# Cross attention: each score tile moved one slot ahead, evictions put before exponents, dense products moved with them

## The reference

```python
# x: (2, 2048, 512), ctx_1024: (2, 154, 512), 16 heads of 32
def _layernorm(x): return (x - mean(x)) / sqrt(var(x) + 1e-5)
q = (_layernorm(x) @ Wq.T + bq)          # heads of 32
k = (ctx @ Wk.T + bk);  v = (ctx @ Wv.T + bv)
attn = softmax(q @ k.T / sqrt(32))       # per head, over 154 keys
x = x + (attn @ v) @ Wo.T + bo
x = x + ffn(_layernorm(x))               # ffn: two layers of local attention + gated MLP
```

## Time and profile before

| | us |
|---|---|
| median of 3 runs | 3729.19 (3726.97 to 3729.65) |
| the profiled execution, its own time | 3725.76 |
| its span, first to last instruction | 3724.0 |
| cross attention groups, about | 63 to 642 of the span |
| TensorE busy over the span | 3486.6 (94%) |

### The profile page before, as it was taken

One profiled execution on the slowest core, in us unless ns is written; L12 is line 12 of the kernel. 1 busy time (PEld: TensorE's weight loads), 2 busy tenths in 40 slices (PEclk: granted clock), 3 DMA queues, 4 the chain that ended last, 5 costly groups with the idle time before them and its releaser, 6 DMA issues. The chain is left out here.

```text
span 3724.0 us, 56508 instructions
## 1 busy us (share of the span) xinstructions
PE 3486.6 (94%) x20624; PEld 2821.9 (76%) x20624; DVE 2267.6 (61%) x5002; ACT 1504.1 (40%) x3973; POOL 1177.3 (32%) x1036
## 2 busy tenths in 40 slices
PE   5889987799999997999999969999999699999998
PEld 4666665688888875888888858888888588888887
DVE  5776775699999984322332239999999642322221
ACT  4655663455555553111111125555555421111111
POOL 2333342555555531111111125555555111111111
PEclk8999999899999998999999989999999899999999
DMA  5111122212121114111111121211111231111111
GB/s 132 39 42 54 56 76 70 92 61 64 60 63 58 58 51 139 66 63 63 63 63 62 52 103 51 63 59 58 58 58 56 89 112 62 63 63 63 63 62 52
DMA packets 215591, 249.21 MB, mean 67 GB/s; under 512 B 32761, under 2 KB 142594, under 8 KB 215317
## 3 DMA queue, kind: packets, MB, share of 16 engines
q1 hardware_dynamic: 215317, 245.61, 20.3%
HBM read 138.17 MB, written 90.61 MB: 61 GB/s over the span
## 5 line engine op out<-in xcount | busy, mean ns | idle before, releaser
L1674 DVE SCALAR_TENSOR_TENSOR u_full<-banks,b_cols,gate 128x512 f32<-128x512 f32 (+1 forms) x176 | 132.1, 751 | 890.8 <-ACT gate L1616 793.2
L45 PE MATMUL banks<-fxT_h,w_h 128*128 128x512 f32 (+1 forms) x1408 | 558.3, 397 | 5.2 <-DVE fxT_l L1666 5.2
L47 PE MATMUL banks<-fxT_h,w_l 128*128 128x512 f32 (+1 forms) x1408 | 557.3, 396 | 0.0
L46 PE MATMUL banks<-fxT_l,w_h 128*128 128x512 f32 (+1 forms) x1408 | 556.5, 395 | 0.0
L1616 ACT ACTIVATE gate<-banks,b_cols 128x512 f32<-128x512 f32 (+1 forms) x176 | 121.3, 689 | 1028.8 <-PE banks L47 1028.8
L1010 POOL TENSOR_TENSOR rn<-ssq,neg_half 128x8 f32<-128x8 f32 x128 | 210.8, 1647 | 410.7 <-DVE ssq L1282 404.2
L45 PE MATMUL banks<-wqkv_h,hT_h 128*128 128x512 f32 x768 | 323.3, 421 | 16.1 <-DVE wqkv_l L1269 16.1
L1323 DVE TENSOR_SCALAR prob<-prob,rc 128x384 f32<-128x384 f32 (+2 forms) x512 | 315.6, 658 | 9.1
L45 PEld LDWEIGHTS banks<-fxT_h,w_h 128*128 128x128 f32 (+1 forms) x1408 | 260.3, 185 | 75.7 <-DVE fxT_l L1666 11.1
L1218 ACT ACTIVATE pT_h<-banks 128x384 fp32r<-128x384 f32 (+2 forms) x512 | 213.7, 469 | 254.3 <-PE banks L1107 253.5
L47 PEld LDWEIGHTS banks<-fxT_h,w_l 128*128 128x128 f32 (+1 forms) x1408 | 261.2, 186 | 67.6
(11 more groups left out here) (170 smaller groups left out, 8195.4 us busy)
## 6 DMA issues: line engine op xcount, KB each, us to landing
y_in<-y_rows SPq DMA_DIRECT2D x64, 256.0 KB, 2.9
z_rows<-y_in SPq DMA_DIRECT2D x64, 256.0 KB, 2.0
f_res<-z_rows SPq DMA_DIRECT2D x16, 1024.0 KB, 5.6
f_x<-x_rows SPq DMA_DIRECT2D x16, 1024.0 KB, 8.0
y_rows<-f_res SPq DMA_DIRECT2D x16, 1024.0 KB, 4.3
out_rows<-f_x SPq DMA_DIRECT2D x16, 1024.0 KB, 4.8
w_ffn_stage<-in_w SPq DMA_DIRECT2D x30, 512.0 KB, 4.9
x_in<-in_x SPq DMA_DIRECT2D x10, 1024.0 KB, 6.7
```

The source lines that it names most:

```text
L45: pe.matmul(out, a_h, b_h, start=start, stop=False)
L46: pe.matmul(out, a_h, b_l, start=False, stop=False)
L47: return pe.matmul(out, a_l, b_h, start=False, stop=stop)
L1674: e.scalar_tensor_tensor(out=u_full[r, m % 2, :], in0=ps[r, 2 * (m % 2), :], scalar=b1[r, m, 0:1], in1=gate[r, :], op0=ALU.add, op1=ALU.mu ...
```

## The change

The scores of tile k+1 (not k) of quarter q+1 stand in slot (q, k), and tile 0 of quarter q+2 stands in slot (q, 4) behind the values product, so that the first tile of a quarter comes one slot sooner. The maxima and exponents are moved with them. In each slot ACT now does `hi_q`, `hi_p` and `hi_x` ahead of the exponents; before, the exponents of tile 0 stood ahead of `hi_p`. The dense products are now at Q2 (0,1), P0 at the end of (0,2), P1 (0,3), P2 (0,4), P3 (1,0), Q3 (1,2), TX0 at the end of (1,3), TX1 at the end of (1,4), TX2 at the end of (2,0), TX3 (2,1), Q0 (2,2), Q1 (3,2). On DVE, normalise moves to (0,1) and (0,2), moments to (3,2) and (3,4), and all four finish instructions stand together at (1,2). SP sends the first half of the second batch's keys ahead of the stores of that group. No instruction is added or taken away in the groups.

```diff
@@ -397,11 +397,13 @@
                 def body(g, s):
                     if g.first:
                         return
+                    if s == XSLOTS - 1:
+                        e.wait_ge(pe_s, NS * g.it + GT * K_HALVES[0][1])
+                        load_keys(1, 0)
                     store_before(g, g.it)
                     if s == XSLOTS - 1:
-                        for half, (_, c1) in enumerate(K_HALVES):
-                            e.wait_ge(pe_s, NS * g.it + GT * c1)
-                            load_keys(1, half)
+                        e.wait_ge(pe_s, NS * g.it + GT * K_HALVES[1][1])
+                        load_keys(1, 1)
                         for half, (_, c1) in enumerate(V_HALVES):
                             e.wait_ge(pe_o, DC * g.it + c1)
                             load_values(1, half)
@@ -547,33 +549,24 @@
                     for q in range(DC):
                         for k in range(QK):
                             m = QK * q + k
-                            if k < GT and not (g.last and q == DC - 1):
-                                if (q, k, s) == (DC - 1, 0, XSLOTS - 1):
-
-                                    e.wait_ge(ld_k[0], g.turn * K_LOADED + 2 * K_LOADED)
-                                if (q, k) == (1, 0):
-                                    reloaded(ld_k[1], K_LOADED)
-                                scores(it, q + 1, k)
+                            if k < GT - 1 and not (g.last and q == DC - 1):
+                                scores(it, q + 1, k + 1)
                             transpose_p(it, m)
-                            if (q, k) == (0, 1) and not g.first:
-
-                                e.wait_ge(dv_o, DC * it)
-                                project(0, TURNS, q_out(2))
-                            elif (q, k) == (0, 2) and not g.first:
+                            if (q, k) == (0, 1):
+                                queries(2, q_out(2))
+                            elif (q, k) == (0, 3) and not g.first:
...
                                 values(it, m - 2)
@@ -582,8 +575,22 @@
                                 if k == 2 and q in (0, DC - 1):
                                     reloaded(ld_v[q // (DC - 1)], V_LOADED)
                                 values(it, m - 2)
-                            if (q, k) == (1, 4) and not g.last:
+                            if k == GT and not (g.last and q >= DC - 2):
+
+                                if (q, s) == (DC - 2, XSLOTS - 1):
+                                    e.wait_ge(ld_k[0], g.turn * K_LOADED + 2 * K_LOADED)
+                                if q == 0:
+                                    reloaded(ld_k[1], K_LOADED)
+                                scores(it, q + 2, 0)
+                            if (q, k) == (0, 2) and not g.first:
+                                e.wait_ge(dv_o, DC * it)
+                                project(0, TURNS, q_out(3))
+                            elif (q, k) == (1, 3) and not g.last:
                                 transpose_x(it + 1, 0, TURNS, q_out(4))
+                            elif (q, k) == (1, 4) and not g.last:
+                                transpose_x(it + 1, 1, TURNS, x_out(1))
+                            elif (q, k) == (2, 0) and not g.last:
+                                transpose_x(it + 1, 2, TURNS, x_out(2))
 
                 def nothing():
                     pass
@@ -598,6 +605,7 @@
                 queries(1, nothing)
                 scores(0, 0, 2)
                 scores(0, 0, 3)
+                scores(0, 1, 0)
                 for half in ld_v:
                     e.wait_ge(half, V_LOADED)
                 run(e, body)
@@ -641,19 +649,18 @@
                     for q in range(DC):
                         more = not (g.last and q == DC - 1)
                         for k in range(QK):
-                            if k == 0 and q != 2 and more:
-                                exps(it, q + 1, k)
                             if k == 1 and not (g.first and q == 0):
                                 hi_o(it, q - 1)
+                            if k == (2 if q == 0 else 3) and (q < 2 or not g.last):
+                                hi_q(it, q + 2)
                             hi_p(it, QK * q + k)
-                            if (q, k) == (1, 4) and not g.last:
-                                hi_x(it + 1, 0, TURNS)
-                            elif q == 2 and k < 3 and not g.last:
-                                hi_x(it + 1, k + 1, TURNS)
-                            if (0 < k < GT or (q, k) == (2, 0)) and more:
-                                exps(it, q + 1, k)
-                            if k == 3 and (q < 2 or not g.last):
-                                hi_q(it, q + 2)
+                            x_of = {(1, 3): 0, (1, 4): 1, (2, 0): 2, (2, 1): 3}.get((q, k))
+                            if x_of is not None and not g.last:
+                                hi_x(it + 1, x_of, TURNS)
+                            if k < GT - 1 and more:
+                                exps(it, q + 1, k + 1)
+                            if k == GT and not (g.last and q >= DC - 2):
+                                exps(it, q + 2, 0)
...
@@ -761,37 +769,32 @@
                         more = not (g.last and q == DC - 1)
                         for k in range(QK):
 
-                            x1_of = {(0, 2): 0, (0, 3): 1, (1, 0): 2, (1, 1): 3}.get((q, k))
+                            x1_of = {(0, 3): 0, (0, 4): 1, (1, 0): 2, (1, 1): 3}.get((q, k))
+                            x_of = {(1, 3): 0, (1, 4): 1, (2, 0): 2, (2, 1): 3}.get((q, k))
                             if x1_of is not None and old:
                                 add_x1(it - 1, g.slot(-1), x1_of, TURNS)
-                            if k == 1 and q == 0 and old:
+                            if k == (2 if q == 0 else 3) and (q < 2 or not g.last):
+                                lo_q(it, q + 2)
+                            if k < GT - 1 and more:
+                                maxima(it, q + 1, k + 1)
+                            if k == 1 and (q or old):
                                 lo_o(it, q - 1)
                             if k < GT and more:
-                                maxima(it, q + 1, k)
-                            if k == 1 and q:
-                                lo_o(it, q - 1)
-                            if 0 < k < GT and more:
-                                recip(it, q + 1, k - 1)
+                                recip(it, q + 1, k)
                             lo_p(it, QK * q + k)
-                            if k == 3:
-                                if more:
-                                    recip(it, q + 1, 3)
-                                if q < 2 or not g.last:
-                                    lo_q(it, q + 2)
-                            if (q, k) == (1, 4) and not g.last:
-                                lo_x(it + 1, 0, TURNS)
-                            elif q == 2 and k < 3 and not g.last:
-                                lo_x(it + 1, k + 1, TURNS)
-                            if (q, k) in ((0, 4), (1, 2)) and not g.last:
-                                normalise(it + 1, g.slot(1), (0, 1) if q == 0 else (2, 3))
-                            y_of = {(0, 2): 0, (0, 4): 1, (1, 0): 2, (1, 1): 3}.get((q, k))
-                            if y_of is not None and old:
-                                moments_y(it - 1, g.slot(-1), y_of)
-                            if (q, k) in ((1, 3), (1, 4)) and old:
-                                for tt in ((0, 1) if k == 3 else (2, 3)):
+                            if x_of is not None and not g.last:
+                                lo_x(it + 1, x_of, TURNS)
+                            if k == GT and not (g.last and q >= DC - 2):
+                                maxima(it, q + 2, 0)
+                            if (q, k) in ((0, 1), (0, 2)) and not g.last:
+                                normalise(it + 1, g.slot(1), (0, 1) if k == 1 else (2, 3))
+                            if x1_of is not None and old:
+                                moments_y(it - 1, g.slot(-1), x1_of)
+                            if (q, k) == (1, 2) and old:
+                                for tt in range(GT):
                                     finish(it - 1, g.slot(-1), tt)
-                            if q == DC - 1 and k in (0, 2) and not g.last:
-                                moments(g.slot(2), g.round(2), (0, 1) if k == 0 else (2, 3))
+                            if (q, k) in ((DC - 1, 2), (DC - 1, 4)) and not g.last:
+                                moments(g.slot(2), g.round(2), (0, 1) if k == 2 else (2, 3))
                     assert g.last or own[0] == (OWN_FIRST if g.first else OWN), own[0]
```

More of the change, by code:

```diff
@@ L306, in cross_phase @@
     LEAD = 1 + GT
-    OWN_BEFORE, OWN_FIRST, OWN = 2 * LEAD + GT, LEAD + NS, LEAD + NS + 2 * GT
+    OWN_BEFORE, OWN_FIRST, OWN = 2 * LEAD + GT + 1, LEAD + NS, LEAD + NS + 2 * GT
```

(24 more changed lines are left out.)

2 lines of the change are left out of this document (removed).

## The result

| | before | after |
|---|---|---|
| median of 6 runs, us | 3729.42 | 3710.30 (3708.53 to 3713.32) |
| profiled execution's own time | 3725.76 | 3710.49 |
| its span | 3724.0 | 3708.7 |
| one inner group | 71.6 | 68.6 (four of six), 70.5 and 70.7 (two) |

The ratio is 0.9950 (95% interval 0.9937 to 0.9963): 19 us faster, where 20 us was forecast. The cross attention alone gave 19.5 us (the next phase's first TensorE row came at 656.68 us and now comes at 637.20), so that in this one pair of profiles the unchanged rest was about 4 us longer. That is inside the scatter of this part: over the profiles of all fourteen kernels here it takes 3065.3 to 3074.2 us, whatever the cross attention did.

The account below looks back on a forecast made before the run. TensorE was taken as busiest but stalled on PSUM banks not yet emptied, with a slowed clock. Gaining 3.8 us and losing 1.1 gives 2.7 us per group, 20 in all: 3729.2 to 3709 us, range 3688 to 3740.

Parts of the forecast that it names:

- The sum: Per inner group, 3.8 us gained in Stretch A less 1.1 lost in Stretch B: 2.7 us, 20 us in all.
- Stretch A: Q0's start to Q3's end, 56.4 us: 6.2 us taken away less 2.4 of new waits, a gain of 3.8 us.
- What the change takes away: In Stretch A, moved products cover bank waits: 4.5 us of stalls and 1.7 of slow clock go, 6.2 us.
- the prediction's cover by Q2: In Stretch A, P0's 1.34 us wait for `lo_o` goes because Q2 now stands ahead.
- What is late next: New waits in Stretch A: 0.9 us at (3,2), 1.0 at P0, 0.5 at P1, together 2.4 us.
- Stretch B: Q3's end to Q0's start, an eviction chain of 15.2 us: between 15.2 and 17.3, taken as 16.3, a 1.1 us loss.
- the slow clock: In Stretch B, about 2.1 us idle ahead of TX0 lowers the clock over TX0, TX1 and scores between: + 0.8 us.
- The finish lump: In Stretch B, the four finish instructions on DVE, 1.8 us, can lose up to 0.9 us beside a POOL divide.
- Given back: Rival, chance 0.15: Stretch B loses 2.1 us, Stretch A gains 2.5; 0.4 us per group, 3726 us, no change.
- slower: Rival, chance 0.17: row evictions ahead of exponents in (1,4), (2,0), (2,1) lengthen Stretch B by 5.9 us; 3744 us.
- All of it: Rival, chance 0.15: no collisions, Stretch A's waits 1.4 us, Stretch B 15.1; 4.9 us per group, 3693 us.

Follow-up runs that it names:

- run 5: Changed kernel with ACT doing exponents ahead of the probability eviction in slot 0 of all four quarters: 3748.8 us, ratio 1.0050 to the kernel before.
- run 6: Changed kernel with exponents ahead of the probability eviction in slot 0 of all quarters, and Q1 back in (3,3): 3755.6 us, ratio 1.0070 to the kernel before.
- run 3: Changed kernel with Q1 alone back in (3,3): 3708.6 us, ratio 0.9952 to the kernel before.
- run 4: Kernel before with one edit: in slot 0 ACT does the probability eviction ahead of the exponents; 3713.1 us, ratio 0.9964.
- run 2: Scores, maxima and exponents one slot earlier, probability evictions ahead of exponents, dense products at their old places: 3727.4 us, ratio 0.9998 to the kernel before.
- Runs 4 and 9: Run 4 has its own line; 9 is run 4 with Q1 in (3,2) and no lead of the scores: 3715.8 us, ratio 0.9962 to the kernel before.
- runs 1 and 2: Run 2 has its own line; 1 has the change's products, layer-norm steps and evictions, but scores, maxima, exponents in old slots: 3731.9 us, 1.0008 to before.
- Runs 7 to 12: On the changed kernel, 7, 8, 11, 12 cumulatively move add_x1, finish, Q2/Q3 evictions, normalise: 3698.9, 3695.2, 3688.4, 3685.4 us; 10, kernel before with moments later: 3729.9 us.

## Why the prediction was right, and where it was not

- *Time.* 3709 forecast, 3710.3 measured. The sum came out right, but partly by luck: the new waits were put too low, and what TensorE saves in busy time too low as well, and the two errors nearly cancel.
- *Stretch A* (Q0's start to Q3's end) was to fall from 56.4 to 52.6 us. It fell to 53.15. The clock is 1.00 in four of six groups, as forecast, and 0.96 in the same stretch of one of the other two (249.40 to 304.57, 55.2 us). Of the 3.2 us, 2.8 are less busy time, where the sum had 1.7, all of it for the clock; idle time fell by 0.4 us, where the sum had 4.5 less 2.4.
- *The price of the cover was wrong.* The step "What the change takes away" says that Q1 with its 2.8 us stands between and hides the wait for `lo_o`. It can: run 5, with late evictions, has no such wait over 0.2 us in its inner groups, and run 6, without Q1 there, has 0.85 us in (3,2). But it is not what was needed: run 3 took that cover away and nothing came back, and run 4 brought 16 us with no product moved, as ACT evicts before it does exponents and DVE comes to `lo_o` two microseconds sooner. I had the swap in front of me and priced its gain at nothing. For P0 the prediction's cover by Q2 may well count once the scores have their lead: in run 2, with both back in their old places, P0 waits 1.90 us for `lo_o` although the evictions stand in front.
- *What is late next* was sized well for P0 (1.0 forecast, 0.82), P1 (0.5, 0.41) and the scores of (3,1) and (3,2) (0.9, 0.32 + 0.69). Missing were P3's 1.50 us and two of 0.26 and 0.37 us (a transpose, a score tile), so that the new waits are 4.4 us and not 2.4. For P3 I looked for who frees the bank, not for what stands ahead of that instruction on DVE.
- *Stretch B*: from TX0 to Q0 I walked 11.9 us; it is 11.84 (376.83 to 388.67). With Q3 to TX0, 15.5 us against 16.3 forecast and 15.2 before. Idle time rose by 1.8 us, as feared; the slow clock for which 0.8 us were charged is not there (0.89 before, 1.00 after), and that pays for most of it. The finish lump did what was feared: four instructions took 2.45 us, by the prediction's estimate 1.8 alone, with a divide beside them:

```profile
373.57 2.45 DVE L762 TENSOR_SCALAR y_t<-x_in,y_mv,y_rs 128x512 f32<-128x512 f32 x4
```

```profile
373.15 1.21 POOL L438 TENSOR_TENSOR x_prob<-x_prob,x_rc 128x616 f32<-128x616 f32 x1
```

- *Rivals.* "Given back" and "slower" did not come: B grew by 0.3 us. The mechanism of the latter, evictions ahead of exponents as a cost, had the wrong sign where it was tried: at (2,0), run 5, the opposite order raised TX3's wait from 0.61 to 2.10 us. No run reverses the row evictions of (1,4) and (2,1). "All of it" needed waits of 1.4 us in A, and they are 4.4.
- *Open.* Runs 4 and 9 came to 3713.1 and 3715.8 us, and runs 1 and 2, which have the same order of evictions, to 3731.9 and 3727.4. So the order is not enough under every placement; how much the changed kernel loses by the old order alone stays open, as run 5 reversed (2,0) too. What the lead and the products add on top of run 4 is 3 us of medians, or 5 us by the ratios, and the intervals overlap; in the profiled executions it is nothing (636.5 and 637.2 us). Runs 7 to 12 build on them and gain more, but no such series was tried on run 4. And what lowers the clock in one group and not in the next, with the same idle times, no run shows.

## What to carry to other kernels

Where an engine does both the emptying of a bank and long work that nobody waits for yet, let the emptying go first, and look two engines on: the stall showed not as busy ACT, which had spare time, but as a wait of DVE behind it. On an engine that works in order, ask of each wait what stands behind it: in the kernel after, the last matmul of P2 began at 359.46 us, yet its addition began at 362.97, behind maxima that could not start before 361.23 and a pair of moments. Check a wait's removal by the sum: a wait may go as worked out and come back one place later. And read idle time and clock apart: here TensorE stood still longer after the change and the group was still 3 us shorter, because its clock stayed up.

## What the runs showed of the hardware that I had not expected

- The same kernel in its steady groups had Q0 at clock 0.50 in two and at 1.00 in the others, with TX0, the scores, TX3 and Q0 at the same distances to 0.02 us in the two groups compared, and about 2 us between the two kinds of group.
- DVE's `tensor_scalar` instructions, with one SBUF input and none in PSUM, did not end before POOL was nearly done when they began beside a divide or the add of the bias: negated maxima up to 1.25 us for 0.17, a normalise pair 1.54 for 0.99, four of finish 2.45 for an estimated 1.8. Beside POOL's small power (128x4) the negated maxima kept their 0.17 us. The evictions, which read PSUM, and the moments kept their time beside any of them.
- The Trainium skill (GPSIMD Engine Reference, Specifications) states contention between GpSimd and VectorE for VectorE instructions in a two-port mode or with two SBUF inputs. These rows agree that there is one; the slowed instructions have one SBUF input, so of the two cases only the first can be theirs, and no row shows an instruction's mode.
